# Two score units back to back, PSUM banks shared with the outputs, and a new order on every engine

## The chip, the cores and the metric

The kernel runs on one core of a Trainium2 chip. Its time is the device time of one execution in microseconds (us); the figure for a kernel is the median of its runs. Five engines work on it, each through its own queue in order: TensorE (PE, matmuls, which read SBUF and write the eight PSUM banks), VectorE (DVE), ScalarE (ACT), GpSimd (POOL) and SyncE (SP, which here issues all the transfers). They wait for each other by semaphores only: an instruction that waits holds up everything behind it in its engine's queue.

## The reference

`x` is 8 x 1024 x 512 in float32. The kernel adds to it an attention and a small feed-forward network, both of its layer norm:

```python
xn = _layernorm(x)
Q, K, V = xn @ Wq + bq, xn @ Wk + bk, xn @ Wv + bv        # 16 heads of 64
scores = einsum('bhid,bhjd->bhij', Q, K)
columns = where(|i - j| <= 64, scores, 0.0)               # 0, not -inf
out = softmax(columns) @ V                                # then @ Wo + bo
s = xn @ Win + bin_                                       # 64 columns
g = sum_h relu(s * W1[:, h] + b1[:, h]) * W2[:, h] + b2   # 16 of them
x + attention + (g @ Wout + bout)
```

Outside the band the score is 0 and still takes part in the softmax. So the kernel subtracts the mean of V, computes a window of 256 columns per 128 rows, and corrects by the equal weight.

## The kernel before, in words

A batch has 1024 tokens (8 tiles of 128) and 16 heads, taken in 8 pairs; two heads fill the 128 partitions. The unit of the schedule is a **step**, one pair of one batch, 64 of them, about 36 us each. In step n PE does three things in turns: the projections to V, Q and K of pair n (`project`, 12 matmuls of 512 columns each for a half of the tokens, six halves), the attention of pair n-1 (`scores`, `transpose_weights`, `weigh_values`), and the output projection of pair n-2 (`project_out`, 8 tiles of three matmuls). Each product is made of three passes over a high and a low part of its operands, so that float32 accuracy is kept in fp32r; ACT writes the high part out of PSUM, then DVE subtracts it from PSUM for the low part, and only then is the bank free.

`scores(tp)` covers two tiles of tokens. Its matmuls contract over the 64 rows of one head, so the two heads run side by side in the 64*128 shape of the array (twelve matmuls, in six couples, into one bank per head). All else on PE has the 128*128 shape. So each call is a visit to the other shape: in at its first matmul, out after its last. A step has four calls.

The eight PSUM banks before: `fill0` and `fill1` for projections, output tiles and values; `score0` and `score1`; `pT_ps0` and `pT_ps1` for the transposed weights; `o_ps0` and `o_ps1` for the outputs of a unit (one head, one half of the tokens; units u = 0 to 3). `OUT_BANK` and `QK_BANK` are tables that say which of the two fill banks an output tile or a projection of Q or K takes.

Per step the others do this. DVE masks the scores and takes their row maximum (`mask_scores`), ACT takes the exponentials (`exps`), DVE the denominators, POOL normalises the weights (`normalise_weights`), PE transposes them (`transpose_weights`), ACT and DVE split them (`weights_high`, `weights_low`), PE applies them to V (`weigh_values`), ACT and DVE sum the two parts of the outputs (`output_half`, `output_sum`). DVE adds each output tile to `acc` (`add_output`). The first two pairs of each batch carry the feed-forward network too, the last two the layer norm and transposes of the next batch. The four middle pairs are a loop on every engine; they are called plain steps here.

The order on each engine is the order in which its `step` is written, by hand; there is no scheduler. A bank is guarded by a wait in front of the matmul that writes it next. Stages are named below by their calls: V0, V1, Q0, Q1, K0, K1 for the projections' halves, out0 to out7 for the output tiles, TW and PV with a unit's number for `transpose_weights` and `weigh_values`, TV0 and TV1 for `transpose_values`.

## Time and profile before

| | before |
|---|---|
| runs | 2547.38 us (median of 3; 2533.61 to 2549.32) |
| span of the profiled execution | 2553.6 us |
| PE busy | 2428.0 us, 95% |
| DVE, ACT, POOL busy | 1987.7, 1701.5, 1208.9 us |
| PE on the chain that ended last | 71% of the span |
| mean granted clock of PE | 0.987 |

The profiled execution's time is known only by its span, from the first to the last instruction; it lies 4 us above the highest of the three runs. In a timeline row the start and the duration of a matmul are given; matmuls overlap in the pipeline, so what one costs PE is the distance from its start to the next one's start, not its duration. "Idle before" with "<-" names what the engine had waited for. PEclk is the granted clock, 1.00 for 2.4 GHz and 0.50 for 1.2 GHz, averaged over the window. Engines other than PE are idle a fifth of the time or more, so a wait on them matters only where it holds PE.

### The profile page before, as it was taken

The page shows a single profiled execution, that of the slowest core. Times are in us where ns is not written, and L with a number is a line of the kernel's source. Part 1 is how long each engine was busy: PE and PEld are TensorE (multiplying, and loading weights), DVE is VectorE, ACT ScalarE, POOL GpSimd, SP SyncE. Part 2 cuts the span into 40 slices and gives each one's busy share as a digit, 9 for nine tenths or more (in the row PEclk, how much of TensorE's full clock was granted, in tenths as well). Part 3 has the DMA queues.
Part 4 walks back from the last instruction along what each step waited for, and adds up shares of the span by engine and source line. Part 5 has one row for each costly group of instructions (what it writes and reads, how often), then busy time and mean ns, then how long its engine had stood idle before and what let it go on. Part 6 is the DMA issues. An engine that isn't in the chain of part 4 may idle for free.

```text
span 2553.6 us, 50140 instructions
## 1 busy us (share of the span) xinstructions
PE 2428.0 (95%) x14913; PEld 2006.8 (79%) x14913; DVE 1987.7 (78%) x5025; ACT 1701.5 (67%) x4458; POOL 1208.9 (47%) x1515
## 2 busy tenths in 40 slices
PE   4999999999999999999999999999999999999997
PEld 3788787888778787787877878778887788878886
DVE  3777888778887788777887777877779778797777
ACT  3666776667766677666775667756677666766665
POOL 2444445445454454544454444544546444464443
PEclk9999999999999999999999999999999999999999
DMA  3010112110121110201103011031010210012101
GB/s 118 22 30 20 34 30 87 33 34 18 34 83 33 34 29 23 92 24 34 34 17 100 21 30 34 17 100 33 18 34 19 98 33 30 22 52 65 33 21 38
DMA packets 130239, 106.04 MB, mean 42 GB/s; under 512 B 5736, under 2 KB 104064, under 8 KB 130048
## 3 DMA queue, kind: packets, MB, share of 16 engines
q1 hardware_dynamic: 130048, 103.72, 13.3%
q8 instruction: 92, 1.51, 0.3%
q14 instruction: 99, 0.81, 0.1%
HBM read 86.93 MB, written 16.78 MB: 41 GB/s over the span
## 4 chain that ended last, share of the span: by engine, by line
PE 71%; DVE 7%; issue 6%; ACT 6%; DMA 4%; POOL 3%; SPq 1%; DVEq 0%; ACTq 0%; POOLq 0%
PE fill L811 33%; PE fill L822 12%; PE o_ps L884 9%; PE pT_ps L867 7%; PE score L803 5%; ACT probs L382 3%; DMA w_raw<-in_L_attn_Wv 2%; DVE probs L594 2%; DMA out_x<-acc 2%; POOL acc L314 1%; POOL probs L301 1%; PE fill L856 1%; PE fill L849 1%; PE pT_ps L841 1%; ACT v L439 1%
## 5 line engine op out<-in xcount | busy, mean ns | idle before, releaser
L301 POOL TENSOR_SCALAR probs<-probs,inv_l,neg_e 128x256 f32<-128x256 f32 x1024 | 598.7, 598 | 778.6 <-DVE neg_e L609 778.6
L811 PE MATMUL fill<-xT_hi,w_hi 128*128 128x512 f32 x1536 | 627.0, 408 | 26.3 <-ACT vT L404 6.7
L382 ACT ACTIVATE probs<-probs,neg_max 128x256 f32<-128x256 f32 x1024 | 510.8, 501 | 154.1 <-DVE neg_max L599 152.4
L811 PE MATMUL fill<-xT_lo,w_hi 128*128 128x512 f32 x1536 | 608.5, 396 | 0.0
L811 PE MATMUL fill<-xT_hi,w_lo 128*128 128x512 f32 x1536 | 605.9, 394 | 0.0
L615 DVE TENSOR_TENSOR acc<-fill,acc 128x512 f32 (+1 forms) x512 | 350.6, 685 | 100.8 <-PE fill L822 93.6
L594 DVE CUSTOM_DVE_ANT_0 probs<-score,mask 128x256 f32<-128x256 f32 x1024 | 372.5, 421 | 33.6 <-issue 20.6
L811 PEld LDWEIGHTS fill<-xT_hi,w_hi 128*128 128x128 f32 x1536 | 293.7, 191 | 108.7 <-issue 26.6
L420 ACT ACTIVATE pT_hi<-pT_ps 128x512 fp32r<-128x512 f32 x512 | 278.2, 592 | 137.4 <-PE pT_ps L867 137.4
L307 POOL TENSOR_TENSOR oT_lo<-o_sum,oT_hi 128x512 fp32r<-128x512 f32 x128 | 171.1, 1337 | 411.3 <-ACT oT_hi L434 411.3
L811 PEld LDWEIGHTS fill<-xT_hi,w_lo 128*128 128x128 f32 x1536 | 292.5, 190 | 65.4
L811 PEld LDWEIGHTS fill<-xT_lo,w_hi 128*128 128x128 f32 x1536 | 293.6, 191 | 56.1
L637 DVE TENSOR_TENSOR pT_lo<-pT_ps,pT_hi 128x512 fp32r<-128x512 f32 x512 | 327.9, 682 | 1.4 <-ACT pT_hi L420 1.3
L884 PE MATMUL o_ps<-pT_hi,v 128*128 128x256 f32 (+1 forms) x1280 | 307.8, 279 | 0.0
L884 PE MATMUL o_ps<-pT_lo,v 128*128 128x256 f32 (+1 forms) x1280 | 305.5, 279 | 0.0
L867 PEld LDWEIGHTS pT_ps<-ident,probs 128*128 128x128 f32 x2048 | 242.8, 142 | 47.2 <-DVE pT_lo L637 9.8
L867 PE MATMUL pT_ps<-ident,probs 128*128 128x128 f32 x2048 | 273.5, 277 | 6.3 <-DVE pT_lo L637 4.8
L280 POOL TENSOR_TENSOR w_lo<-w_raw,w_hi 128x512 fp32r<-128x512 f32 x192 | 248.0, 1292 | 52.6 <-ACT w_hi L349 52.6
L822 PE MATMUL fill<-wo_hi,oT_hi 128*128 128x512 f32 x512 | 233.9, 457 | 32.1 <-DVE acc L615 21.6
L884 PEld LDWEIGHTS o_ps<-pT_lo,v 128*128 128x128 f32 x1280 | 243.2, 190 | 2.6
L884 PEld LDWEIGHTS o_ps<-pT_hi,v 128*128 128x128 f32 x1280 | 242.5, 189 | 2.6
L630 DVE SCALAR_TENSOR_TENSOR qT_lo<-fill,bias_qkv,qT_hi 128x512 fp32r<-128x512 f32 x128 | 95.8, 748 | 147.2 <-ACT qT_hi L412 147.2
(104 smaller groups left out, 4252.2 us busy)
## 6 DMA issues: line engine op xcount, KB each, us to landing
w_raw<-in_L_attn_Wv SPq DMA_DIRECT2D x64, 256.0 KB, 3.3
w_raw<-in_L_attn_Wq SPq DMA_DIRECT2D x64, 256.0 KB, 3.7
w_raw<-in_L_attn_Wk SPq DMA_DIRECT2D x64, 256.0 KB, 2.7
acc<-in_L_attn_x SPq DMA_DIRECT2D x8, 2048.0 KB, 9.3
wo_raw<-in_L_attn_Wo SPq DMA_DIRECT2D x64, 256.0 KB, 2.8
out_x<-acc SPq DMA_DIRECT2D x7, 2048.0 KB, 7.7
acc<-in_L_attn_x SPq DMA_DIRECT2D x2, 1024.0 KB, 6.7
out_x<-acc SPq DMA_DIRECT2D x2, 1024.0 KB, 4.3
```

Source lines behind the costliest of these rows:

```text
L280: pool.tensor_tensor(w[lo][:, i], w_raw[:, i], f32(w[hi][:, i]), ALU.subtract).then_inc(w_lo, 1)
L301: pool.tensor_scalar(probs[:, h, t], probs[:, h, t], inv_l[:, c:c + 1], neg_e[:, c:c + 1], ALU.mult, ALU.add).then_inc(normed, 1)
L307: pool.tensor_tensor(oT[lo][:, cols], o_sum[half][:], f32(oT[hi][:, cols]), ALU.subtract) \
L382: act.activation(probs[:, h, t], probs[:, h, t], ACT.Exp, bias=neg_max[:, c:c + 1], accum_out=row_sum[:, c:c + 1])
L420: act.activation(pT[u % 2][hi][:, k * LINE:k * LINE + LINE], pT_ps[k][:], ACT.Copy) \
L594: dve.tensor_tensor_reduce(out=probs[:, h, t], in0=score[h][:, i * WIN:i * WIN + WIN], in1=mask[:], scale=1.0, scalar=0.0, op0=ALU.mult, o ...
L615: dve.tensor_tensor(acc[:, parity, t], bank[:], acc[:, parity, t], ALU.add).then_inc(out_added, 1)
L637: dve.tensor_tensor(pT[u % 2][lo][:, cols], pT_ps[k][:], f32(pT[u % 2][hi][:, cols]), ALU.subtract).then_inc(pT_lo, 1)
L811: last = pe.matmul(dst[:], w[wp][:, i, k], xT[xp][:, k, half * LINE:half * LINE + LINE], start=(k == 0 and a == 0), stop=(k == KC - 1 and ...
L822: last = pe.matmul(dst[:], oT[op][:, t * P:t * P + P], wo[wp][:], start=(a == 0), stop=(a == 2))
L867: last = pe.transpose(pT_ps[k][:, i % 4 * P:i % 4 * P + P], probs[:, h, t, c * P:c * P + P], ident[:])
L884: last = pe.matmul(o_ps[h][:, q0:q0 + (end - first) * P], v[:, (4 * half + k) % T, h].rearrange("p a d -> p (a d)"), pT[h][part][:, first ...
```

## The change

The four score banks are now shared: `attn0` to `attn3` take the scores of tp 0 (banks 0, 1), tp 1 (2, 3), tp 2 (0, 1) and tp 3 (2, 3), and the outputs of units 0 to 3. `scores(0)` and `scores(1)` stand back to back, as do `scores(2)` and `scores(3)`. The tables of fill banks are new, and the order of the calls in the `step` of PE, ACT and DVE is written anew; POOL and SP keep theirs. No instruction of arithmetic is added or taken away.

```diff
-        score = [bank("score0"), bank("score1")]
+        attn = [bank(f"attn{i}") for i in range(4)]
+        score = [[attn[2 * i + h] for h in range(2)] for i in range(2)]
+        o_ps = attn
-        OUT_BANK = (1, 0, 0, 0, 1, 0, 0, 0)
-        QK_BANK = (1, 0, 1, 1)
+        OUT_BANK = (1, 1, 1, 1, 0, 1, 0, 0)
+        QK_BANK = (0, 1, 0, 1)
...
# DVE, step
                 if attend:
                     mask_scores(0)
+                    mask_scores(1)
...
                 if out_proj:
                     add_output(5)
                 if proj:
                     qk_low(2)
-                if attend:
-                    weights_low(2)
-                    output_sum(1)
                 if out_proj:
                     add_output(6)
+                if attend:
+                    weights_low(2)
...
-                if out_proj and not ln_next:
-                    add_output(7)
+                if attend:
+                    output_sum(2)
                 if proj:
                     qk_low(3)
                 if ln_next:
                     x_low(b + 1, range(0, 2))
+                if out_proj:
                     add_output(7)
                 if attend:
-                    output_sum(2)
+                    output_sum(3)
...
# PE, scores(tp)
-                    if begun(16 * j + 4 * tp):
-                        pe.wait_ge(masked, 16 * j + 4 * tp)
+                    if tp >= 2:
+                        pe.wait_ge(masked, 16 * j + 4 * tp - 4)
+                    elif begun(4 * j + 2 * tp - 2):
+                        pe.wait_ge(o_summed, 4 * j + 2 * tp - 2)
...
# PE, step
                 if attend:
                     scores(0)
+                    scores(1)
...
-                if attend:
-                    scores(1)
                 if out_proj and not proj:
                     project_out_last(1)
                 elif out_proj:
-                    pe.wait_ge(v_in, 2 * n + 1)
+                    pe.wait_ge(out_added, T * o + 1)
                     project_out(1)
...
                 elif out_proj:
                     pe.wait_ge(qk_lo, 4 * n + 2)
                     project_out(5)
-                if attend:
-                    transpose_weights(2)
-                    weigh_values(1)
                 if out_proj and not proj:
                     project_out_last(6)
                 elif out_proj:
-                    pe.wait_ge(out_added, T * o + 6)
+                    pe.wait_ge(qk_lo, 4 * n + 3)
                     project_out(6)
                 if attend:
                     transpose_weights(3)
+                    weigh_values(2)
```

Three places of the plain step follow, as the compiled program has them. In the names the number behind `fill`, `pT_ps`, `score` or `attn` is the bank; "waits" names semaphores: `out_added` counts DVE's additions of output tiles, `qk_lo` its subtractions for Q and K, `pT_lo` those for the transposed weights. `REGISTER_ALU` and `ISA` rows only set up or make a wait.

**PE between out0 and out1.** Before, out0's last matmuls, then the scores; out1 came after them, into `fill0`:

```order
L822 MATMUL fill1<-wo_hi,oT_hi 128x512 [waits oT_lo]
L822 MATMUL fill1<-wo_lo,oT_hi 128x512
L822 MATMUL fill1<-wo_hi,oT_lo 128x512
L797 REGISTER_ALU
L803 MATMUL score0<-kT_hi,qT_hi 128x256 [waits masked]
```

Now:

```order
L814 MATMUL fill1<-wo_hi,oT_hi 128x512 [waits oT_lo]
L814 MATMUL fill1<-wo_lo,oT_hi 128x512
L814 MATMUL fill1<-wo_hi,oT_lo 128x512
L913 ISA
L814 MATMUL fill1<-wo_hi,oT_hi 128x512 [waits out_added]
```

out1 takes the same bank as out0, directly behind it, and waits for out0's addition.

**PE from out5 or out6 to TW3.** Before, the end of PV1, then out6 and TW3 (TW2 and PV1 stand between out5 and out6):

```order
L884 MATMUL o_ps1<-pT1_hi,v 128x128
L884 MATMUL o_ps1<-pT1_lo,v 128x128
L996 REGISTER_ALU
L822 MATMUL fill0<-wo_hi,oT_hi 128x512 [waits out_added]
L822 MATMUL fill0<-wo_lo,oT_hi 128x512
L822 MATMUL fill0<-wo_hi,oT_lo 128x512
L862 REGISTER_ALU
L866 REGISTER_ALU [waits normed]
L867 MATMUL pT_ps0<-ident,probs 128x128 [waits pT_lo]
```

Now:

```order
L814 MATMUL fill1<-wo_lo,oT_hi 128x512
L814 MATMUL fill1<-wo_hi,oT_lo 128x512
L985 REGISTER_ALU
L814 MATMUL fill0<-wo_hi,oT_hi 128x512 [waits qk_lo]
L814 MATMUL fill0<-wo_lo,oT_hi 128x512
L814 MATMUL fill0<-wo_hi,oT_lo 128x512
L854 REGISTER_ALU
L858 REGISTER_ALU [waits normed]
L859 MATMUL pT_ps0<-ident,probs 128x128 [waits pT_lo]
L859 MATMUL pT_ps0<-ident,probs 128x128 x3
L858 REGISTER_ALU
L859 MATMUL pT_ps1<-ident,probs 128x128 [waits pT_lo]
```

out6 stands directly behind out5 and waits for the subtraction of K0 out of `fill0`; TW3 stands directly behind out6 and waits for the subtraction of unit 2's weights out of `pT_ps0`.

**DVE at the same place.** Before, from the addition of out5 on:

```order
L615 TENSOR_TENSOR acc<-fill0,acc 128x512 [waits out_done]
L629 REGISTER_ALU
L630 ISA [waits qk_hi]
L630 SCALAR_TENSOR_TENSOR kT_lo<-fill1,bias_qkv,kT_hi 128x512
L636 REGISTER_ALU
L637 TENSOR_TENSOR pT0_lo<-pT_ps0,pT0_hi 128x512 [waits pT_hi]
L636 REGISTER_ALU
L637 TENSOR_TENSOR pT0_lo<-pT_ps1,pT0_hi 128x512 [waits pT_hi]
L647 SCALAR_TENSOR_TENSOR o_sum0<-o_ps1,v_back,o_part1 64x512 [waits v_back_ready,o_half]
L613 REGISTER_ALU
L615 TENSOR_TENSOR acc<-fill0,acc 128x512 [waits out_done]
```

Now:

```order
L612 TENSOR_TENSOR acc<-fill1,acc 128x512 [waits out_done]
L626 REGISTER_ALU
L627 ISA [waits qk_hi]
L627 SCALAR_TENSOR_TENSOR kT_lo<-fill0,bias_qkv,kT_hi 128x512
L610 REGISTER_ALU
L612 TENSOR_TENSOR acc<-fill0,acc 128x512 [waits out_done]
L633 REGISTER_ALU
L634 TENSOR_TENSOR pT0_lo<-pT_ps0,pT0_hi 128x512 [waits pT_hi]
L633 REGISTER_ALU
L634 TENSOR_TENSOR pT0_lo<-pT_ps1,pT0_hi 128x512 [waits pT_hi]
```

The addition of out5 still comes ahead of K0's subtraction; the addition of out6 has moved ahead of the two subtractions of unit 2's weights.

## Rows read from the trace of the kernel before

**Rows 1.** the page: the span of the profiled execution.

```profile
span 2553.6 us, 50140 instructions
```

**Rows 2.** one plain step; columns: window, length, PE, PEld, DVE, ACT, POOL, PEclk, DMA, GB/s.

```profile
493.10:528.90 35.80, 35.56 (x226) 29.68 (x225) 27.52 (x73) 23.86 (x67) 16.73 (x22) 1.00 0.10 29
```

**Rows 3.** timeline of PE: one scores visit; start us, us, engine, line, operation, [idle before].

```profile
502.23 0.39 PE L811 MATMUL fill<-xT_hi,w_lo 128*128 128x512 f32 x1
502.55 0.39 PE L803 MATMUL score<-kT_hi,qT_hi 64*128 64x256 f32 x2
...
503.45 0.50 PE L822 MATMUL fill<-wo_hi,oT_hi 128*128 128x512 f32 x1
503.79 0.40 PE L822 MATMUL fill<-wo_lo,oT_hi 128*128 128x512 f32 x1
504.03 0.40 PE L822 MATMUL fill<-wo_hi,oT_lo 128*128 128x512 f32 x1
```

**Rows 4.** timeline, last step: PE waits for DVE's addition out of one bank.

```profile
2541.72 0.40 PE L822 MATMUL fill<-wo_hi,oT_lo 128*128 128x512 f32 x1
...
2542.15 1.39 DVE L615 TENSOR_TENSOR acc<-fill,acc 128x512 f32<-128x512 f32 x2 [0.38 <-PE fill L822]
...
2542.90 0.50 PE L822 MATMUL fill<-wo_hi,oT_hi 128*128 128x512 f32 x1
```

**Rows 5.** timeline, end of a plain step: PE, ACT and DVE around the last keys.

```profile
560.49 0.39 PE L811 MATMUL fill<-xT_hi,w_lo 128*128 128x512 f32 x1
...
560.99 0.69 ACT L412 ACTIVATE kT_hi<-fill,bias_qkv 128x512 fp32r<-128x512 f32 x1 [1.64 <-PE fill L811]
561.17 0.39 PE L822 MATMUL fill<-wo_hi,oT_lo 128*128 128x512 f32 x1
...
561.59 0.69 DVE L615 TENSOR_TENSOR acc<-fill,acc 128x512 f32 x1 [1.74 <-PE fill L822]
...
562.20 0.74 DVE L630 SCALAR_TENSOR_TENSOR kT_lo<-fill,bias_qkv,kT_hi 128x512 fp32r<-128x512 f32 x1
```

**Rows 6.** timeline of DVE: the two subtractions that free pT_ps0 and pT_ps1.

```profile
547.05 1.29 DVE L637 TENSOR_TENSOR pT_lo<-pT_ps,pT_hi 128x512 fp32r<-128x512 f32 x2
```

**Rows 7.** timeline of PE: outputs of one unit, then one output tile, then transposes.

```profile
519.41 0.30 PE L884 MATMUL o_ps<-pT_hi,v 128*128 128x128 f32 x1
...
520.60 0.45 PE L822 MATMUL fill<-wo_hi,oT_hi 128*128 128x512 f32 x1
...
521.35 0.38 PE L867 MATMUL pT_ps<-ident,probs 128*128 128x128 f32 x2
```

**Rows 8.** waits of PE: operation, releaser, us in total, times, longest us.

```profile
PE fill L822 <- DVE acc L615: 21.6, 7, 3.1
...
PE fill L822 <- DVE qT_lo L630: 9.4, 7, 1.8
```

**Rows 9.** timeline of DVE, a batch's first pair: the subtraction of the values' mean.

```profile
673.85 4.02 DVE L731 TENSOR_SCALAR vT<-vT,v_new 128x1024 f32<-128x1024 f32 x1
```

**Rows 10.** groups of DVE by line: count, busy us, mean ns, idle before.

```profile
L623 DVE SCALAR_TENSOR_TENSOR xn<-xn,w2c 128x1024 f32<-128x1024 f32 x56 | 74.6, 1332 | 2.1 <-ACT xn L392 0.9
```

**Rows 11.** timeline of PE: two long waits, and the matmuls after the second.

```profile
1998.26 1.03 PE L867 MATMUL pT_ps<-ident,probs 128*128 128x128 f32 x8
2001.08 0.49 PE L822 MATMUL fill<-wo_hi,oT_hi 128*128 128x512 f32 x1 [1.78 <-DVE qT_lo L630]
...
2516.05 0.39 PE L803 MATMUL score<-kT_hi,qT_hi 64*128 64x256 f32 x2 [1.99 <-DVE row_max L594]
...
2517.46 0.63 PE L822 MATMUL fill<-wo_lo,oT_hi 128*128 128x512 f32 x1
2517.89 0.63 PE L822 MATMUL fill<-wo_hi,oT_lo 128*128 128x512 f32 x1
```

**Rows 12.** busy time by window around those two waits; columns as in Rows 2.

```profile
1998.20:2002.20 4.00, 2.22 (x14) 1.75 (x13) 2.00 (x7) 2.79 (x10) 0.63 (x1) 1.00 0.00 0
2512.90:2521.00 8.10, 5.86 (x36) 3.94 (x33) 6.02 (x24) 5.56 (x21) 1.27 (x1) 0.79 0.04 14
```

More of the change, by code:

```diff
@@ L485, in step @@
                     copied.then_inc(ffn_half, 1)
+                if ln_next:
+                    normalise(b + 1, range(2, 4))
                 if attend:
+                    weights_high(1)
                     exps(3)
-                if proj and not ffn_first:
+                    output_half(0)
+                if proj:
                     qk_high(1)
                 if attend:
-                    weights_high(1)
-                    output_half(0)
-                if proj and ffn_first:
-                    qk_high(1)
+                    output_half(1)
                 if ffn_first or ffn_last:
@@ L731, in step @@
                     dve.tensor_scalar(vT[:], vT[:], v_new[:], None, ALU.subtract).then_inc(v_centered, 1)
+                    qk_low(0)
+                for half in range(2) if ffn_first else ():
+                    line = slice(half * LINE, half * LINE + LINE)
+                    dve.wait_ge(ffn_half, 2 * b + half + 1)
+                    dve.scalar_tensor_tensor(ffn_s[:, line], fill[1 - half][:], ffn_bin[:], ffn_part[:, line],
+                                             ALU.add, ALU.add).then_inc(ffn_s_in, 1)
+                if attend:
+                    weights_low(1)
+                if out_proj:
+                    add_output(4)
+                if attend:
+                    denominators(1)
+                    output_sum(0)
+                if proj:
+                    qk_low(1)
+                if attend:
+                    output_sum(1)
+                if ffn_first or ffn_last:
+                    hidden(0 if ffn_first else 6)
                 if out_proj:
@@ L802, in scores @@
                                 rows = slice(h * D, h * D + D)
-                                last = pe.matmul(score[h][:, i * WIN:i * WIN + WIN], qT[qp][rows, t * P:t * P + P],
+                                last = pe.matmul(score[tp % 2][h][:, i * WIN:i * WIN + WIN], qT[qp][rows, t * P:t * P + P],
                                                  kT[kp][rows, t * P:t * P + WIN], start=(a == 0), stop=(a == 2))
@@ L883, in weigh_values @@
                         for part in (hi, lo):
-                            last = pe.matmul(o_ps[h][:, q0:q0 + (end - first) * P],
+                            last = pe.matmul(o_ps[u][:, q0:q0 + (end - first) * P],
                                              v[:, (4 * half + k) % T, h].rearrange("p a d -> p (a d)"),
@@ L1022, in step @@
                         pe.wait_ge(out_added, T * o + T)
+                    else:
+                        pe.wait_ge(qk_lo, 4 * n + 3)
                     transpose_values(0)
```

155 lines of the change are left out of this document (62 added, 93 removed).

## The prediction

> **What bounds the kernel now.** I read the page first, then the busy times of one plain step, then PE's timeline in it. The span is 2553.6 us [rows 1]; the runs' median, 2547.38, lies 6 below, and I take 6 off at the end. In a plain step of 35.8 us PE is without work for 35.80 - 35.56 = 0.24 us, while DVE, ACT and POOL have 6 to 19 us to spare [rows 2]. So PE sets the time: each us that it loses or gains in a step is lost or gained 64 times, and work on the others counts only where PE waits for it. The question is therefore what the change does to PE's own work, and what PE meets at each wait in the new order.
>
> **The visits to the 64-row shape.** From the last matmul before a visit to the second one after it pass 504.03 - 502.23 = 1.80 us [rows 3]. Without changes of shape it would be one slot of 0.23, six couples of 0.117 (two matmuls of 256 columns at a time, half a 512-column slot of 0.23 each) and two slots of 0.23: 1.39. A visit costs 0.41: the way in, a slow first couple, the way out, and a first matmul that takes 0.34 instead of 0.23 [rows 3]. Two visits of four go in each of 64 steps: 128 x 0.41 = **-52**. The wait of 0.24 ahead of V0 in a plain step [rows 2] goes as well, since V0 now starts a visit's length later: some 20 steps, **-5**.
>
> **out1 behind out0.** Both use `fill1`, and nothing stands between them. The last step has this very pattern: PE's last matmul into a bank starts at 2541.72, DVE's addition at 2542.15, and PE may write the bank again at 2542.90 [rows 4]. That is 1.18 from start to start where a slot is 0.23, a stall of 0.95; the matmul after it is slow as after a visit (0.34 for 0.23), 0.10 more. DVE is there in time: counted from scores(0), I estimate that it starts on the maskings at 1.9 us, after the values of the step before, and is through both at 5.0 (about 1.55 each), while out0's last matmul ends at 5.3. 1.05 in the 55 steps that have output tiles and do not put transposes of x in between: **+58**. In two steps of each batch DVE has a 128x1024 instruction of 1.33 us [rows 10] or two statistics ahead of that addition, 0.8 us late: 14 x 0.8 = **+11**. The cover that the old order had was the visit of scores(1).
>
> The Trainium skill, TensorEngine Tiling, PSUM Bottleneck, says that tiling speeds up TensorE but not the evacuation of PSUM. By it the two maskings, now one behind the other in front of out0's addition, would make that stall longer in every step; by the 0.3 us of room above they don't, and the sum stays.
>
> **out6 behind out5.** Its bank, `fill0`, holds K0, and DVE reaches K0's subtraction only after out5's addition. So PE waits for out5's own addition and then the subtraction. The old end of a step has this pair on DVE: last matmul of a tile 561.17, addition 561.59, subtraction 562.20, lasting 0.74 [rows 5], 1.77 in all, and 0.06 to PE's next matmul (2542.15 and 0.69 of the first addition to 2542.90 [rows 4]). 1.83 - 0.23 + 0.10 for the slow start = 1.70, in 62 steps: **+105**. Before, TW2, PV1 and their 2 us stood between.
>
> **TW3 behind out6.** `pT_ps0` still holds unit 2's weights, whose subtraction stands on DVE behind the addition of out6. 0.42 to the addition, 0.61 until the next instruction can start [rows 5], then 0.68 for the first of a couple that takes 1.29 [rows 6], and 0.06: 1.77 - 0.23 = 1.54. The second half waits for `pT_ps1`, 0.61 later, with 0.44 of transposes meanwhile: 0.17. 1.71 in 62 steps: **+106**. Before, one PV and one tile, 521.35 - 519.41 = 1.94 [rows 7], lay ahead of TW3, and the subtraction ahead of the addition.
>
> **TV0 behind K1, out7 and PV3.** It needs out7's addition, now behind K1's subtraction. From K1's last matmul: 0.50 to ACT, 0.69 there, then DVE 0.03 + 0.61 + 0.68 and 0.06 [rows 5, 6]: 2.57. PE gets there after 0.23 + 0.75 + 1.19 = 2.17 [rows 5, 7]. 0.40 in 55 steps (where the next batch's transposes stand between, none): **+22**.
>
> **What else moves.** scores(1) waits for the sum of unit 3, which now comes ahead of the values: about 1 us to spare. TW2 needs POOL's weights about 0.1 us before PE is there; between 0 and 0.4 us a step, I take 0. SP and POOL keep their order. At batch ends old waits go. Seven times PE waits 3.1 us for an addition [rows 8] that stands behind a subtraction of 4.02 us [rows 9]; this now runs earlier, while POOL is idle, and nothing like it stands in the way. Seven more of 9.4 us in all, for Q0's subtraction ahead of out4 [rows 8], go too, since Q1 lies between. Together 31 us, and the drop of the clock that follows the long ones, 7 x 1.6 (below): **-42**, at least 0 if others take their place.
>
> **The clock.** After a wait of 1.78 us the granted clock stayed at 1.00; around one of 1.99 it was 0.79 on average [rows 11, 12], with matmuls at 0.43 instead of 0.23 (2517.46 to 2517.89 [rows 11]). The new waits at out6 and TW3 are 1.6 and 1.5 us with 0.69 of matmuls between: neither alone is long enough by these rows, together they are longer than both. No row has such a pair. At best the clock never falls (0), at worst in all 62 steps. A fall to 1.2 GHz lasts for about eight matmuls of 0.43 in the nearest rows and so costs 8 x 0.2 = 1.6. I take half the steps, between rows on either side: 31 x 1.6 = **+50**.
>
> The Trainium skill, TensorE: Matmul & The Clock Gate, PE-mode transpose, says that transposes do not count as busy for the clock. If so, TW2 ahead of the pair and TW3 behind it lengthen the idle stretch. The rows speak against: eight transposes stood ahead of the 1.78 us wait and the clock held [rows 11, 12].
>
> **The sum.** -52 - 5 + 58 + 11 + 105 + 106 + 22 - 42 + 50 = +253. On 2553.6 that is 2806.6, less 6: **2800 us**, a tenth slower. A plain step goes from 35.8 to 39.6, and to 41.2 where the clock falls.
>
> **Rivals.**
> - The clock never falls: 2750 us, chance 0.27. For it: each wait alone is under 1.78. Against: little work lies between them.
> - The clock falls in every step, as a rule that leaves out transposes would have it (the page above): 62 x 1.6 = 99 instead of 50, 2849 us. Chance 0.17. Against it, the 1.78 us wait.
> - The new waits are partly hidden or the batch ends gain more: by DVE's reaching its work earlier than the rows of the old order show, half of the 280 us of waits and little of the clock's: about 2650 us, 0.09. Against it: the chains consist of durations, not of queues.
> - Faster: if DVE answered each of the four waits within the PE work that is still in flight, only the saving of visits and old waits is left: 2553.6 - 52 - 5 - 42 - 6 = 2449 us. It decides from the point at which the four waits of a step together are shorter than 0.8 us plus the batch ends' 0.7; by the rows they are 4.9. Chance 0.02.
> - The change doesn't do what it says: the visits stay at four because the wait between two calls empties the array. scores(1) and scores(3) have such waits, but satisfied ones. The forecast would be 52 higher, 2852; inside the case above and in its chance.
>
> My forecast of 2800 has 0.45, with an own range of 2765 to 2835 (0 to 0.4 us at TW2, 0 to 42 at batch ends). The range for all, 8 in 10: **2715 to 2870**. A difference under 1% can't be told from none here. Faster by over 1% 0.02, within 1% 0.02, slower 0.96.
>
> **What would show it.** Six couples of scores run on into the next six without a slow couple between them, and two visits a step. PE's waits by line: out tiles on `kT_lo`, about 60 times 1.4 us; out tiles on `acc`, some 55 times 0.5 to 0.8; transposed weights on `pT_lo`, about 60 times 1.4. PE busy falls from 95% to 87%, and the slices of PEclk show 8s and 9s at a regular distance. The prediction is wrong if out6 starts within 1 us of out5's last matmul, or if the wait moves to POOL's weights.

## The result: a sixth slower, further than forecast

The changed kernel takes 2950.27 us (median of 4 runs, 2945.26 to 2959.71), the kernel before on the same chip 2541.70 (median of 4, 2533.61 to 2549.32). The ratio is 1.162, with a 95% interval of 1.158 to 1.166. The forecast was 2800 with a range up to 2870: right in sign and too small. The profiled execution rose from 2553.6 to 2958.0 us, by 404 where the sum said 253, so 151 us are to be explained. The kernel before and the changed one differ from run to run by up to 16 us, and with them the mean clock (0.941 to 0.947 in the four runs of the changed one), so small differences are read from single steps below and not from the total.

From the page of the kernel after: the span, PE's and DVE's busy time with their share and their number of instructions, PE's granted clock in 40 slices, and the chain that ended last by engine.

```profile
span 2958.0 us, 49955 instructions
...
PE 2550.4 (86%) x14913; PEld 2102.1 (71%) x14913; DVE 2009.3 (68%) x5025; ACT 1685.4 (57%) x4458; POOL 1157.5 (39%) x1515
...
PEclk9999999999999999999999999999899999999999
...
PE 67%; DVE 17%; issue 10%; ACT 4%; DVEq 1%; SPq 0%; POOL 0%; DMA 0%; ACTq 0%; POOLq 0%
```

PE was busy for 95% of the span and is for 86%. Of the 404 us, 122 stand in its busy time itself (2550.4 against 2428.0), though it has no more matmuls to do: those are matmuls at the low clock. The mean granted clock is 0.941 after 0.987. In 40 slices a fall is averaged away (one 8 among 40, where the forecast wanted 8s at a regular distance), so the next view is by step. Two neighbouring steps; columns as in Rows 2:

```profile
514.57:554.97 40.40, 35.80 (x225) 29.45 (x225) 26.88 (x73) 23.52 (x67) 16.23 (x23) 1.00 0.09 26
554.97:596.90 41.93, 37.78 (x219) 31.45 (x220) 25.86 (x72) 22.77 (x66) 15.47 (x22) 0.92 0.08 25
```

The first step keeps the clock and takes 40.40 us where the step of [rows 2] takes 35.80: PE is without work for 4.60 us instead of 0.24. The second loses the clock for a while and takes 1.5 more. Of the 24 steps of pairs 3 to 5 only two are of the first kind. The mean over these 24 is 42.16.

The waits of PE in the kernel after (released by, us in total, times, longest), which answer to [rows 8]:

```profile
PE fill L814 <- DVE kT_lo L627: 91.0, 62, 1.6
PE pT_ps L859 <- DVE pT_lo L634: 90.6, 64, 1.8
PE fill L814 <- DVE acc L612: 89.2, 64, 3.2
PE fill L848 <- DVE acc L612: 42.3, 55, 1.8
```

These are the four places of the forecast: out6, TW3, out1 (and some others of that kind), TV0. Now each in the timelines.

**The visits.** Timeline of PE, last couples of scores(0), first of scores(1), the way out:

```profile
556.57 0.28 PE L795 MATMUL attn<-kT_lo,qT_hi 64*128 64x256 f32 x2
556.69 0.28 PE L795 MATMUL attn<-kT_hi,qT_lo 64*128 64x256 f32 x2
556.81 0.28 PE L795 MATMUL attn<-kT_hi,qT_hi 64*128 64x256 f32 x2
...
557.62 0.50 PE L803 MATMUL fill<-xT_hi,w_hi 128*128 128x512 f32 x1
557.95 0.40 PE L803 MATMUL fill<-xT_lo,w_hi 128*128 128x512 f32 x1
```

Between 556.69 and 556.81, where one unit's scores end and the next one's begin, the distance is 0.12 as within a unit: no slow couple, no way out and in. Two visits a step are gone, as forecast.

**out6 and TW3.** Timelines of PE and DVE in the step that keeps the clock, to be read beside [rows 4, 5]:

```profile
543.39 0.40 PE L814 MATMUL fill<-wo_hi,oT_lo 128*128 128x512 f32 x1
545.22 0.50 PE L814 MATMUL fill<-wo_hi,oT_hi 128*128 128x512 f32 x1 [1.44 <-DVE kT_lo L627]
...
545.79 0.40 PE L814 MATMUL fill<-wo_hi,oT_lo 128*128 128x512 f32 x1
547.57 1.26 PE L859 MATMUL pT_ps<-ident,probs 128*128 128x128 f32 x8 [1.38 <-DVE pT_lo L634]
```

```profile
543.82 0.69 DVE L612 TENSOR_TENSOR acc<-fill,acc 128x512 f32 x1 [2.11 <-PE fill L814]
544.43 0.74 DVE L627 SCALAR_TENSOR_TENSOR kT_lo<-fill,bias_qkv,kT_hi 128x512 fp32r<-128x512 f32 x1
546.22 0.69 DVE L612 TENSOR_TENSOR acc<-fill,acc 128x512 f32 x1 [1.05 <-PE fill L814]
546.83 1.28 DVE L634 TENSOR_TENSOR pT_lo<-pT_ps,pT_hi 128x512 fp32r<-128x512 f32 x2
```

543.39 to 545.22 is 1.83, and 545.79 to 547.57 is 1.78: less a slot of 0.23 and with the slow start, 1.70 and 1.66, where 1.70 and 1.71 were forecast with the second half of TW3. DVE is idle for 2.11 and 1.05 us ahead of the two additions: its order, not its load, makes these waits. The subtraction of K0 could have been done in those 2.11 us.

**out1.** PE, then DVE, then POOL, in the next step:

```profile
560.92 0.39 PE L814 MATMUL fill<-wo_hi,oT_lo 128*128 128x512 f32 x1
562.63 0.50 PE L814 MATMUL fill<-wo_hi,oT_hi 128*128 128x512 f32 x1 [1.32 <-DVE acc L612]
```

```profile
557.50 1.14 DVE L762 TENSOR_TENSOR v_back<-v_new,bias_qkv 128x1 f32<-128x1 f32 x1
558.57 0.41 DVE L591 CUSTOM_DVE_ANT_0 probs<-attn,mask 128x256 f32<-128x256 f32 x1
...
561.76 0.17 DVE L596 TENSOR_SCALAR neg_max<-row_max 128x4 f32<-128x4 f32 x1
561.89 0.69 DVE L612 TENSOR_TENSOR acc<-fill,acc 128x512 f32 x1
```

```profile
557.34 1.28 POOL L308 TENSOR_TENSOR oT_lo<-o_sum,oT_hi 128x512 fp32r<-128x512 f32 x1 [1.85 <-ACT oT_hi L435]
558.59 1.29 POOL L281 TENSOR_TENSOR w_lo<-w_raw,w_hi 128x512 fp32r<-128x512 f32 x1
```

The addition starts at 561.89, 0.97 after out0's last matmul, where 0.43 was forecast [rows 4]. DVE is late because an addition of 128x1 takes 1.14 us, and it ends when POOL's instruction of 1.28 does. The stall is 1.48 and the slow start 0.12, against 1.05 forecast.

**The clock.** PE in the second step, behind the same two waits:

```profile
585.62 0.50 PE L814 MATMUL fill<-wo_hi,oT_hi 128*128 128x512 f32 x1 [1.44 <-DVE kT_lo L627]
...
587.97 1.97 PE L859 MATMUL pT_ps<-ident,probs 128*128 128x128 f32 x8 [1.38 <-DVE pT_lo L634]
...
592.29 0.63 PE L803 MATMUL fill<-xT_lo,w_hi 128*128 128x512 f32 x1
592.72 0.63 PE L803 MATMUL fill<-xT_hi,w_lo 128*128 128x512 f32 x1
...
594.51 0.40 PE L803 MATMUL fill<-xT_lo,w_hi 128*128 128x512 f32 x1
```

Eight transposes take 1.97 instead of 1.26 and matmuls stand 0.43 apart, until about 594. The clock is recorded as low 75 times, for 3.4 us (47 times), 6.8 us (27) or 3.9 us (once), in all 347 us of the span at 1.2 GHz against 67 before. Below, a low stretch is 3.4 us, so the changed kernel has 102 and the kernel before 20. In 50 of the 62 steps with both waits a fall begins within 1.2 us of TW3's start.

**Batch ends.** PE in a batch's first pair of the kernel after, waits alone:

```profile
1107.48 0.50 PE L814 MATMUL fill<-wo_hi,oT_hi 128*128 128x512 f32 x1 [1.87 <-DVE acc L612]
1109.97 0.77 PE L803 MATMUL fill<-xT_hi,w_hi 128*128 128x512 f32 x1 [1.51 <-DVE xT_lo L658]
...
1149.70 0.52 PE L848 MATMUL fill<-ident,vT 128*128 128x128 f32 x3 [1.27 <-DVE acc L612]
```

The old waits of 3.1 and 1.8 us [rows 8] are gone, and these have come for them. In the second pair PE is idle for up to 2.4 us ahead of out1 and 1.8 ahead of TV0. Over seven batches PE's idle time at out1 of the first pair is 13 us, at V1 there 10, and at TV0 of both pairs, beyond the 0.45 of a plain step, 18: about 41 us that the forecast has not. By position in the batch (pairs 1 to 7, then 0) a step took 37.8, 43.3, 35.7, 35.8, 35.8, 39.0, 37.8, 46.3 us and takes 45.3, 47.8, 42.0, 42.2, 42.3, 47.2, 43.8, 52.9 (each from TV0 to the next TV0): the steps at the batch ends have lost about as much as the plain ones.

### The profile page after: what moved, and what is told of

Read it like the earlier page. It is cut to its first block, busy times and chain, and to the rows that moved or that the text cites. A ratio compares the mean times of both kernels' runs of the same rounds, so it can differ in the third digit from the quotient of the medians.

```text
span 2958.0 us, 49955 instructions
## 1 busy us (share of the span) xinstructions
PE 2550.4 (86%) x14913; PEld 2102.1 (71%) x14913; DVE 2009.3 (68%) x5025; ACT 1685.4 (57%) x4458; POOL 1157.5 (39%) x1515
## 4 chain that ended last, share of the span: by engine, by line
PE 67%; DVE 17%; issue 10%; ACT 4%; DVEq 1%; SPq 0%; POOL 0%; DMA 0%; ACTq 0%; POOLq 0%
PE fill L803 30%; PE fill L814 11%; PE pT_ps L859 8%; PE attn L876 8%; PE attn L795 5%; DVE probs L591 4%; DVE acc L612 3%; DVE pT_lo L634 3%; DVE kT_lo L627 2%; PE fill L848 2%; DVE xn L620 1%; DVE v L650 1%; ACT kT_hi L413 1%; PE fill L841 1%; ACT v L440 1%
## 5 line engine op out<-in xcount | busy, mean ns | idle before, releaser
L302 POOL TENSOR_SCALAR probs<-probs,inv_l,neg_e 128x256 f32<-128x256 f32 x1024 | 567.4, 576 | 1031.3 <-DVE neg_e L606 1031.3
L803 PE MATMUL fill<-xT_hi,w_hi 128*128 128x512 f32 x1536 | 650.5, 424 | 13.6 <-DVE xT_lo L658 11.7
L591 DVE CUSTOM_DVE_ANT_0 probs<-attn,mask 128x256 f32<-128x256 f32 x1024 | 372.5, 419 | 37.6 <-PE attn L795 36.1
L859 PE MATMUL pT_ps<-ident,probs 128*128 128x128 f32 x2048 | 311.2, 299 | 98.3 <-DVE pT_lo L634 90.6
L876 PE MATMUL attn<-pT_hi,v 128*128 128x256 f32 (+1 forms) x1280 | 349.9, 303 | 11.7 <-DVE pT_lo L634 11.6
L876 PE MATMUL attn<-pT_lo,v 128*128 128x256 f32 (+1 forms) x1280 | 343.7, 303 | 0.0
L876 PEld LDWEIGHTS attn<-pT_hi,v 128*128 128x128 f32 x1280 | 275.9, 216 | 25.1 <-DVE pT_lo L634 20.4
L336 POOL TENSOR_TENSOR wo_lo<-wo_raw,wo_hi 128x512 fp32r<-128x512 f32 x64 | 85.6, 1338 | 523.6 <-ACT wo_hi L526 523.6
L814 PEld LDWEIGHTS fill<-wo_hi,oT_hi 128*128 128x128 f32 x512 | 97.0, 189 | 257.3 <-DVE kT_lo L627 117.9
L876 PEld LDWEIGHTS attn<-pT_lo,v 128*128 128x128 f32 x1280 | 275.7, 215 | 4.4
```

What stands on the lines that cost most here:

```text
L302: pool.tensor_scalar(probs[:, h, t], probs[:, h, t], inv_l[:, c:c + 1], neg_e[:, c:c + 1], ALU.mult, ALU.add).then_inc(normed, 1)
L591: dve.tensor_tensor_reduce(out=probs[:, h, t], in0=score[tp % 2][h][:, i * WIN:i * WIN + WIN], in1=mask[:], scale=1.0, scalar=0.0, op0=ALU ...
L803: last = pe.matmul(dst[:], w[wp][:, i, k], xT[xp][:, k, half * LINE:half * LINE + LINE], start=(k == 0 and a == 0), stop=(k == KC - 1 and ...
L814: last = pe.matmul(dst[:], oT[op][:, t * P:t * P + P], wo[wp][:], start=(a == 0), stop=(a == 2))
L859: last = pe.transpose(pT_ps[k][:, i % 4 * P:i % 4 * P + P], probs[:, h, t, c * P:c * P + P], ident[:])
L876: last = pe.matmul(o_ps[u][:, q0:q0 + (end - first) * P], v[:, (4 * half + k) % T, h].rearrange("p a d -> p (a d)"), pT[h][part][:, first ...
```

## The experiments

Each ratio is to the kernel before on the same chip. "Plain step" is that of pairs 3 to 5, without low clock where none is named.

**DVE's order, both places.** The subtraction of K0 ahead of out5's addition, and those of unit 2's weights ahead of out6's:

```diff
# DVE, step
-                if out_proj:
-                    add_output(5)
                 if proj:
                     qk_low(2)
                 if out_proj:
-                    add_output(6)
+                    add_output(5)
                 if attend:
                     weights_low(2)
+                if out_proj:
+                    add_output(6)
```

> The changed kernel with DVE's order mended at two places: K0's subtraction (qk_low(2)) ahead of out5's addition, and unit 2's weights' subtraction ahead of out6's addition. PE's order is untouched. Theory A (the two waits cost their length, 3.5 us a step, and together they make the clock fall, 1.76 us a step on the mean): out6 then waits 0.3 us, TW3 0.7, so about 2.35 x 62 = 146 us of waits go and the clock's 109 with them: about 2695 us, mean clock back at 0.98 or more. Rival B (the clock falls for the other waits of the step, at out1 or at TV0, or for the lower busy share as a whole): only the 146 go, about 2804, clock still near 0.94. Rival C (the chain is not DVE's order, another releaser stands right behind): less than 60 us gained.

Measured: 2769.43 us, ratio 1.092 (1.091 to 1.094). PE's two waits in a plain step:

```profile
515.26 0.50 PE L814 MATMUL fill<-wo_hi,oT_hi 128*128 128x512 f32 x1 [0.24 <-DVE kT_lo L627]
...
516.45 1.25 PE L859 MATMUL pT_ps<-ident,probs 128*128 128x128 f32 x8 [0.23 <-DVE pT_lo L634]
```

1.44 and 1.38 have become 0.24 and 0.23, the plain step 38.0, and no plain step loses the clock. Of the 4.1 us that it gains, 2.4 are waits and 1.8 the clock. The waits at out1 and TV0 are as they were (1.32 and 0.45 us idle), so these two alone don't make the clock fall. The whole gains 0.069 of 2542, 176 us, and misses the expected 2695 by 74, since pairs 0 and 1 gain nothing: 44 of the 55 low stretches left lie there, with new waits of 3.2 (pair 0) and 3.85 us (pair 1) at PV3 for unit 3's subtraction.

**Each place alone.** First the keys:

```diff
-                if out_proj:
-                    add_output(5)
                 if proj:
                     qk_low(2)
+                if out_proj:
+                    add_output(5)
```

> Only the first of the two edits: K0's subtraction ahead of out5's addition. out6 then waits 0.3 us instead of 1.6, TW3 still 1.5. Theory A (it takes both waits to make the clock fall): 81 us of waits and the clock's 109 go, about 2760 us. Rival B (one wait of 1.5 us is enough, or the clock falls for another reason): only 81 us go, about 2870 us, clock near 0.94.

Then the weights:

```diff
-                if out_proj:
-                    add_output(6)
                 if attend:
                     weights_low(2)
+                if out_proj:
+                    add_output(6)
```

> Only the second of the two edits: unit 2's weights' subtraction ahead of out6's addition. TW3 then waits for nothing, out6 still 1.6 us. Theory A (it takes both waits): 1.8 x 62 = 112 us of waits and the clock's 109 go, about 2730 us; the savings of this and of the first edit alone then add up to far more than both edits together give, since the clock is counted in each. Rival B (one wait is enough): 112 us go, about 2840 us, and the savings add up.

Measured: 2827.84 (1.116, 1.114 to 1.118) and 2798.84 (1.104, 1.102 to 1.106). The expected times of theory A, 2760 and 2730, are missed by 68 and 69, again in pairs 0 and 1. Against the change they save 115 and 147 us, 262 together, where both edits at once save 176. Something was counted twice, and most of it is the clock: with either wait gone alone, plain steps that keep the clock take 39.2 and 38.6 us, and only two of 48 lose it. Against the 42.16 of the change these are 3.0 and 3.5 us, where both edits give 4.1; of the 2.4 too many, 1.8 is the clock and 0.6 is wait. With either wait removed the other one alone hardly ever makes the clock fall.

**Idle work in out6's wait.** Five matmuls of 512 columns whose result nobody reads; no other work is changed:

```diff
# PE, step, ahead of project_out(6)
+                    if attend:
+                        pe.wait_ge(masked, 16 * j + 16)
+                        for _ in range(5):
+                            pe.matmul(attn[2][:], wo[hi][:, 0:P], oT[hi][:, LINE:N], start=True, stop=True)
```

> The changed kernel with five more matmuls of 128x512 (wo_hi by oT_hi, into attn2, which is free there) on PE between out5 and the wait of out6; their result is overwritten by PV2 and used nowhere. They take 1.14 us of the 1.6 us that PE waits there, so all waits end when they did and no step's chain changes. Theory A (the clock falls because PE stands idle at out6 and TW3): the clock holds, mean 0.98 or more, and the kernel gets faster by about 109 us although PE does more, about 2840 us. Rival B (the fall has nothing to do with the idle time there): no change, 2950 us, or slower, up to 5 x 0.23 x 62 = 71 us where the wait did not cover them, clock near 0.94.

Measured: 2906.02, ratio 1.147 (1.145 to 1.149). The rest of out6's wait and TW3's, in a step that still fell:

```profile
533.49 0.50 PE L814 MATMUL fill<-wo_hi,oT_hi 128*128 128x512 f32 x1 [0.30 <-DVE kT_lo L627]
...
535.84 1.94 PE L859 MATMUL pT_ps<-ident,probs 128*128 128x128 f32 x8 [1.38 <-DVE pT_lo L634]
```

out6 starts no earlier, yet 38 us are gained, with 62 low stretches for 102. So the clock is a cost of its own beside the waits. Theory A expected 109 and a mean clock of 0.98; it is 0.964. In pairs 3 to 5 seven steps of 24 still fell, with 0.30 us of idle time left at out6 and 1.38 at TW3, where with the wait removed two of 24 did. Filling one wait did not do what removing it did.

**Idle work in both waits.** The same, and five more ahead of TW3:

```diff
# PE, step, ahead of transpose_weights(3)
+                    if proj and out_proj:
+                        for _ in range(5):
+                            pe.matmul(attn[2][:], wo[hi][:, 0:P], oT[hi][:, LINE:N], start=True, stop=True)
```

> The changed kernel with five idle matmuls of 128x512 (overwritten, used nowhere) in the wait of out6 and five more in the wait of TW3, 1.14 us in each of the two waits of 1.6 and 1.5 us. The waits for DVE end when they did. Theory A (idle time on PE at these two places makes the clock fall in every plain step): no stretch at 1.2 GHz is left in the plain steps, each takes 40.4 us, and the kernel gets faster than with one wait filled (1.147 of before): 1.13 to 1.14. Rival B: falls stay, 1.15 or more.

Measured: 2872.39, ratio 1.129 (1.126 to 1.132). PE:

```profile
532.40 1.31 PE L988 MATMUL attn<-oT_hi,wo_hi 128*128 128x512 f32 x5
534.01 0.50 PE L814 MATMUL fill<-wo_hi,oT_hi 128*128 128x512 f32 x1 [0.30 <-DVE kT_lo L627]
...
534.81 1.31 PE L994 MATMUL attn<-oT_hi,wo_hi 128*128 128x512 f32 x5
536.36 1.25 PE L859 MATMUL pT_ps<-ident,probs 128*128 128x128 f32 x8 [0.24 <-DVE pT_lo L634]
```

Every plain step now takes 40.4 us, exactly the step of the change that keeps its clock, with ten matmuls more in it. What is gained, 0.033 of 2542 or 84 us, is clock, since the matmuls do nothing else; 33 low stretches are left, none in pairs 3 to 5.

**The banks mirrored from out1 on**, so that out1 takes the other bank and meets an older addition; V1 now waits for out0's:

```diff
-        OUT_BANK = (1, 1, 1, 1, 0, 1, 0, 0)
-        QK_BANK = (0, 1, 0, 1)
+        OUT_BANK = (1, 0, 0, 0, 1, 0, 1, 1)
+        QK_BANK = (1, 0, 1, 0)
...
# PE, step, ahead of out1
-                    pe.wait_ge(out_added, T * o + 1)
+                    pe.wait_ge(v_in, 2 * n + 1)
...
# the feed-forward's and the values' banks follow; ACT: value_lines(0) ahead of exps(0); TV0 waits for K0's and K1's subtractions
```

> The changed kernel with the two fill banks exchanged from out1 on: out1 takes fill0 (and waits for V0's evacuation by ACT, which now comes ahead of the exponentials) and V1 takes fill1, and so on to the end of the step; TV0 then waits for K1's subtraction and TV1 for out7's addition. The order of PE's and DVE's work is as in the changed kernel. Theory (out1's wait of 1.5 us is that for out0's addition out of the same bank behind two maskings, TV0's of 0.6 that for out7's addition behind K1's subtraction): out1 waits about 0.3, TV0 nothing, 1.9 us less in some 55 steps: about 105 us less, 2840 us; the clock goes on falling at out6 and TW3 in every step, 0.94. Rival (out1 would wait for ACT's evacuation or DVE's late start just as long): under 30 us.

Measured: 2859.37, ratio 1.119 (1.117 to 1.121), 108 us less than the change, where 105 were expected. PE, from out0's last matmul to V1:

```profile
508.42 0.39 PE L814 MATMUL fill<-wo_hi,oT_lo 128*128 128x512 f32 x1
508.91 0.50 PE L814 MATMUL fill<-wo_hi,oT_hi 128*128 128x512 f32 x1
...
510.08 0.50 PE L803 MATMUL fill<-xT_hi,w_hi 128*128 128x512 f32 x1 [0.20 <-DVE acc L612]
```

out0 to out1 is 0.49, so 0.26 above a slot is left there, and 0.49 with the slow start is left at V1; TV0 doesn't wait, but TV1 now does (about 0.2). The waits at out1 and TV0 do come from the shared bank. That the total comes out as expected is in part luck: a plain step that keeps the clock falls from 40.4 to 39.3, so 1.1 us and not 1.9, some 70 us in all, and the rest goes with the clock, which is low for 224 us instead of 347. out6 and TW3 wait as before (1.44 and 1.38), and still five plain steps of 24 keep the clock where two did. So the two waits are not all that decides a fall; what else does is not shown.

**This and the DVE order together.**

> The exchange of banks and both mended places of DVE's order together. If the waits are independent, the first run's 2769 us less 105: about 2665 us. If the exchange uncovers a wait of its own at out6 or TW3, 2700 or more.

Measured: 2718.77, ratio 1.065 (1.063 to 1.067); the plain step is 36.9, against the 38.0 of the first experiment. The expected 2665 is missed by 54. Some 19 of these are the chips: before took 2552 us on this one and 2534 on that of the first experiment. By the ratios the exchange saves 0.028, 70 us, as the plain step has it (1.1 us in 62 steps), where 105 were expected. 44 of the 49 low stretches lie in pairs 6, 0 and 1.

**The best order that was found.** As the last, with PV1 between out5 and out6, DVE and ACT in step with it (`output_half(1)`, `output_sum(1)` later), and `v_back` and `neg_max` in the form of the experiment after this one:

```diff
# PE, step
-                if attend:
-                    weigh_values(1)
...
                     project(K_, 0, qk_proj, fill[1])
...
                     project_out(5)
+                if attend:
+                    weigh_values(1)
```

> A version meant to keep the two visits and lose all four waits: exchanged banks, the two small instructions in the other form, unit 1's outputs (PV1) moved between out5 and out6 on PE, DVE in the order qk_low(2), addition 5, weights_low(2), output_sum(1), addition 6, and ACT with output_half(1) behind weights_high(2) and output_high(0) behind weights_high(3). By the forecast's own terms a plain step is then 35.7 - 0.8 - 0.2 + 0.3 (out1) = 35.0 to 35.2 us against 35.74 before. If the batch ends cost what they did before, about 2500 us; if they cost as in the other variants (some 5 us a batch more), about 2540. It is faster than the kernel before only if the two merged visits are worth their 0.8 us a step.

Measured: 2671.56, ratio 1.046 (1.045 to 1.048), slower than before and 130 to 170 above what was expected. The plain step takes 36.9 us, as in the last experiment, where 35.0 to 35.2 was expected. PE, out4's last matmul and K0:

```profile
534.69 0.39 PE L814 MATMUL fill<-wo_hi,oT_lo 128*128 128x512 f32 x1
535.94 0.49 PE L803 MATMUL fill<-xT_hi,w_hi 128*128 128x512 f32 x1 [0.86 <-DVE acc L612]
```

K0 takes out4's bank in every table here, the mirrored one too, and PV1 stood between them. With PV1 gone from there the round trip of [rows 4] is back, with 0.86 of idle time, at K0 instead of out1, and it eats what out6 and TW3 gain. I had moved a stage without reading what it covered, the same mistake of order that the change makes. What this kernel gains on the last lies at the batch ends, with 27 low stretches for 49.

**The 128x1 addition: its form.** `v_back` and `neg_max` as `scalar_tensor_tensor`, to tell whether the form causes the 1.14 us:

```diff
-                    dve.tensor_tensor(v_back[:], v_new[:], bias_qkv[:, V_, pair], ALU.add)
+                    dve.scalar_tensor_tensor(v_back[:], v_new[:], 1.0, bias_qkv[:, V_, pair], ALU.mult, ALU.add)
# neg_max likewise: -2.0 x row_max + row_max
```

> The changed kernel with two small VectorE instructions in another form with the same result: v_back (tensor_tensor, 128x1) and neg_max (tensor_scalar, 128x4) are written with scalar_tensor_tensor. Theory: v_back takes 1.15 us instead of 0.15 because POOL's TENSOR_TENSOR (oT_lo, 1.28 us) runs at the same time, and delays both maskings and with them out0's addition by 1 us; instructions of the scalar_tensor_tensor kind show no such effect in the trace (0.75 with and without). Then v_back takes 0.2 us, the maskings end at 5.0 instead of 5.9 us after scores(0), and out1's wait is 1.0 instead of 1.5: 0.5 in about 55 steps, 25 us less, about 2920 us. Rival (the small instructions wait for something else, such as the semaphore of the output sum): no change, 2945.

Measured: 2953.10, ratio 1.155 (1.152 to 1.159), out1's stall still 1.48:

```profile
557.05 1.15 DVE L763 SCALAR_TENSOR_TENSOR v_back<-v_new,bias_qkv 128x1 f32<-128x1 f32 x1
```

This form still reads two tensors of SBUF, so it doesn't tell the form from the number of its inputs.

**Its place.** `v_back` ahead of the values' subtractions:

```diff
                 if proj:
+                    dve.tensor_tensor(v_back[:], v_new[:], bias_qkv[:, V_, pair], ALU.add)
                     values_low(0)
                     values_low(1)
...
-                    dve.tensor_tensor(v_back[:], v_new[:], bias_qkv[:, V_, pair], ALU.add)
```

> One look, for durations: the changed kernel with v_back (DVE, 128x1) computed ahead of the two subtractions for the values instead of behind them, when POOL runs nothing. Theory (a small VectorE instruction with all its operands in SBUF takes about 1 us longer while POOL's TENSOR_TENSOR of oT_lo or w_lo runs): v_back falls from 1.15 to 0.15 us, and neg_max of the first masking, which then ends inside POOL's next instruction, rises from 0.17 to about 1.0; out1's wait falls by some 0.2 only. Rival (v_back waits for something of its own): it stays at 1.1 us wherever it stands, neg_max at 0.17.

Measured: 2916.70, a single run. DVE:

```profile
509.20 0.16 DVE L759 TENSOR_TENSOR v_back<-v_new,bias_qkv 128x1 f32<-128x1 f32 x1
...
512.11 0.93 DVE L596 TENSOR_SCALAR neg_max<-row_max 128x4 f32<-128x4 f32 x1
514.57 0.69 DVE L612 TENSOR_TENSOR acc<-fill,acc 128x512 f32 x1
```

With POOL idle it takes 0.16. The maskings start 1.07 earlier, but now the first `neg_max` runs beside POOL and takes 0.93 instead of 0.17. Even so out1's stall is 1.03 with DVE's addition 0.53 behind the last matmul: the forecast's 0.95, once DVE is there in time.

**Its inputs.** A tensor and a scalar per partition, in the old place:

```diff
-                    dve.tensor_tensor(v_back[:], v_new[:], bias_qkv[:, V_, pair], ALU.add)
+                    dve.tensor_scalar(v_back[:], v_new[:], bias_qkv[:, V_, pair], None, ALU.add)
```

> The changed kernel with the 128x1 addition that makes v_back written as a tensor with a scalar per partition (v_new, plus the column of bias_qkv) instead of a tensor with a tensor; it stays where it is on VectorE. Theory A (an instruction of DVE with two tensors in SBUF waits for GpSimd's TENSOR_TENSOR that is running, one with a single tensor of one element does not): v_back takes 0.15 us instead of 1.14, the maskings start 1.0 earlier, the first neg_max behind them now runs beside GpSimd and takes 0.9 to 1.0 as in the kernel with v_back moved; out1's wait falls from 1.48 to 1.03 and the time to 2917 us, by a ratio of about 1.146. Theory B (any small instruction with SBUF alone on both sides waits, whatever its form): v_back stays at 1.15, the wait at 1.48, the ratio at 1.16.

Measured: 2917.42, ratio 1.150 (1.146 to 1.154). DVE, and the group of `neg_max` (count, busy us, mean ns):

```profile
511.60 0.20 DVE L762 TENSOR_SCALAR v_back<-v_new,bias_qkv 128x1 f32<-128x1 f32 x1
...
L596 DVE TENSOR_SCALAR neg_max<-row_max 128x4 f32<-128x4 f32 x256 | 86.9, 339 | 8.9
```

The same work in the same place takes 0.20 for 1.14, and PE's idle time ahead of out1 falls from 1.32 to 0.86. A plain step that keeps the clock takes 39.9 for 40.4, some 26 us in 55 steps; what the total gains beyond that goes with the clock, which ten plain steps of 24 keep where two did. `neg_max` rises from a mean of 231 ns to 339, as in the last experiment. The Trainium skill, SBUF — State Buffer, Who interferes with whom, says that an instruction of VectorE with two inputs in SBUF contends with a GpSimd instruction that reads SBUF, and one with a single input doesn't outside the modes that use both ports. The trace agrees for `v_back` (1.14 and 1.15 with two inputs, 0.20 with one and a scalar), and for the instructions that read PSUM, which keep 0.41, 0.69 and 0.75 beside POOL. `neg_max` has one input of four elements and still waits; that it is in such a mode is not shown.

**The instructions ahead of out0's addition** at the batch ends: `hidden(3)` and two statistics moved behind `add_output(1)`.

```diff
# DVE, step
-                if ffn_last:
-                    hidden(3)
-                if stats_next:
-                    statistics(b + 1, range(0, 2))
                 if out_proj:
                     add_output(0)
...
                     add_output(1)
+                if ffn_last:
+                    hidden(3)
+                if stats_next:
+                    statistics(b + 1, range(0, 2))
```

> The changed kernel with VectorE's hidden(3) (the 128x1024 instruction of 1.33 us in the step before a batch's last) and the first two statistics of the next batch moved from ahead of add_output(0) to behind add_output(1). Theory A (out1 waits longer in these two steps of a batch because these instructions stand ahead of the addition): out1's wait there falls from 2.55 and 1.8 to about 1.5, together 1.0 to 1.4 us a batch and whatever of the clock falls with them; 7 to 12 us less, a ratio of 1.157 to 1.159. Rival (something else sets these waits, or what is moved makes out2 or the next unit late): under 3 us.

Measured: 2931.08, ratio 1.157 (1.153 to 1.161), which the noise doesn't tell from the change's 1.162. The waits do tell: in pair 1 PE's idle time ahead of out1 falls from 2.4 to 1.2 in five batches (in the other two it was 0.8), and in sum those behind output additions (third and fourth row of PE's waits above) from 131.5 to 119.8 us. So of the term of +11 the half for pair 1 was real. In pair 6, where the statistics stand, out1's idle time is 0.97 in both kernels, less than a plain step's 1.32: there the term was nothing. Part is handed on: PE now waits for POOL's weights, 0.36 in pair 1 and 0.73 in pair 6, 14.7 us in all for 7.1.

**One visit more.** The first experiment with scores(3) back behind out3:

```diff
                 if attend:
                     scores(2)
-                    scores(3)
...
                     project_out(3)
+                if attend:
+                    scores(3)
```

> The first run's kernel (both of DVE's places mended, 1.0923 of before) with one merged visit taken apart again: scores(3) behind out3 instead of directly behind scores(2). Theory: one visit of 0.41 us more in 64 steps, and no new wait: 26 us slower than that run, a ratio of 1.102 to before. Rival (the merged visit saves nothing there, since a wait for DVE sets the step's end): the ratio stays at 1.092.

Measured: 2789.11, ratio 1.095 (1.093 to 1.098). Each plain step takes 38.40 instead of 38.03, 0.37 for the visit's 0.41. The ratio rises by 0.003 only, where 0.41 x 62 would be 0.010; the medians and the profiled spans of the two differ by 20 us. The plain step is the sharper measure.

**One merged visit in the kernel before**, without the rest of the change:

```diff
# kernel before; PE, step
                     scores(2)
+                    scores(3)
# its scores go to the banks of the outputs; PV0 waits until they are masked
```

> The kernel before with one of the change's ideas alone: scores(3) moved directly behind scores(2), into the two banks of the outputs (o_ps0, o_ps1), which are free there; PV0 waits for its masking. Nothing else on any engine is moved, and between any two writes of one fill bank PE keeps other work. Theory (a visit costs 0.41 us and the change's loss is all in its order, not in sharing banks or in merged visits): one visit of 0.41 less in 64 steps, 26 us, a ratio of 0.990. Rival (the merged couples or the shared banks cost something of their own, or a wait takes its place, such as TW0 reaching POOL's weights earlier): 1.000 or above.

Measured: 2562.64, ratio 1.007 (1.005 to 1.009): slower by under a percent, where 0.990 was expected. PE's waits of this kernel:

```profile
PE fill L825 <- DVE qT_lo L630: 28.9, 43, 2.2
PE fill L825 <- DVE acc L615: 21.5, 7, 3.1
```

The visit's 0.41 is gone, and out4 is in its stead early for the subtraction of Q0: 43 waits of 28.9 us where [rows 8] has 7 of 9.4. The visit had been cover. The plain step goes from 35.7 to 35.9.

## Why the prediction was wrong

- **Visits, V0's wait: right.** 0.41 a visit was forecast; the seam has no slow couple, and splitting one visit again costs 0.37. PE's waits of the kernel after have none at V0 in a plain step.
- **out6, TW3: right**, to 0.1 us, shown by taking each away (38.0 with both of DVE's places mended).
- **out1: mechanism right, mis-sized.** 1.60 instead of 1.05 a step. The failing step is "DVE is there in time: counted from scores(0), I estimate that it starts on the maskings at 1.9 us". It starts at 2.6, since `v_back` takes 1.14, and the two maskings take 3.3 for 3.1, so the 0.3 us of room were not there. The profile before has the mean of `v_back` as 171 ns, in 62 of 64 cases beside no instruction of POOL. The new place and the two inputs are the cause; 0.55 x 55 = 30 us.
- **TV0: mis-sized**, 0.61 for 0.40, some 12 us; with the rest of TW3 the waits together make 0.86 us a step more than forecast by its terms (0.8 by the step, 40.40 for 39.6), about 50 us.
- **The clock: mis-sized, the worst term.** "I take half the steps" at 1.6 us; it was 22 of 24 plain steps, at a mean of 1.76 over all (42.16 less 40.40), 109 us for 50. The rival "falls in every step" had this nearly right, and with it the forecast would have been 2849, inside the range and still 101 short. What showed the mechanism are the two kernels with one wait removed, which keep the clock but for two steps, and that with both waits filled. The argument "neither alone is long enough, together they are longer than both" was right; to halve it was no reading of a row. The Trainium skill, TensorE: Matmul & The Clock Gate, PE-mode transpose, would have transposes not count for the clock; no run tells whether they do, since each experiment leaves TW2 and TW3 where they are.
- **Batch ends: failed.** -42 was forecast. The two old waits went, as said, but about 41 us of waits at out1, V1 and TV0 came in these same steps, and 47 of the 102 low stretches lie in pairs 6, 0 and 1. The floor "at least 0 if others take their place" was in the text, and 0 should have been the value taken: I had costed what the new order removes there, and not walked PE through it.
- 50 + 59 + 42 = 151, the size of the missing time. The first two rest on the plain step and are checked by experiments there; the third is a remainder, and that it fits to the us is chance: the terms are means of plain steps times 55 or 62. The own range, 2765 to 2835, does not follow from the two terms named for it either, which both only add.

**Open:** whether the batch ends can be mended (the best order still loses 2 to 4 us a step in pairs 0, 1 and 6); why one filled wait still lets the clock fall in some steps where the removed one hardly does; why, with both waits in place, the clock held in 2 of 24 plain steps of the change and in 1 to 10 of 24 where something else was changed; why some falls last 6.8 us and others 3.4. No kernel here beats the kernel before.

## What to carry to other kernels

Before two stages on PE are pushed together for a saving between them (here 0.41 us), list for each stage the bank that it writes and what stands on the evacuating engine ahead of the instruction that frees it: what was between them was cover, and waiting for such a bank cost 0.95 to 1.7 us here. Count the clock with the waits: after two waits of 1.4 us with 0.7 of matmuls between, it cost 1.8 us a step more, as much as one of them. And walk every kind of step through the new order, not the plain one alone.

## What was not expected of the hardware

- A DVE addition of 128x1 with two inputs in SBUF takes 1.14 us beside a running TENSOR_TENSOR of POOL and 0.15 to 0.17 otherwise; with one input and a scalar 0.20 beside it. In the kernel before the same cost lay on `neg_max`, 1.06 us in 48 of 256 cases.
- With one of the two waits removed, the other (1.44 or 1.38 us) left the clock at 2.4 GHz in 46 of 48 plain steps; with both in place it held in 2 of 24. Ten matmuls without use made the kernel 78 us faster by medians (2950.27 to 2872.39).
- 64-row couples of different units follow each other at 0.12 us as within a unit.
